# Group-norm statistics of five samples: two small matrix products replaced by a store, a spread load and VectorE sums

## What is computed

```
# per sample; x, ctx: (512, 2048); q = layernorm(x)
t = Wt @ ctx;  p = Wp @ q;  g = Wg @ ctx
# 8 groups of 64 channels
att = sum over the group's channels and columns of p * g     # one number a group
y   = Wz_group @ (att * t_group)
mu, var = mean and variance of y over the group's 64 channels and 2048 columns
x  = x + (y - mu) * rsqrt(var + eps) * gn_w + gn_b + ctx
# feed-forward: layernorm over columns, rows gathered by a permutation,
# 16 heads: gelu(rows @ up[h]) @ down[h], scattered back and added
out = x + ffn(layernorm(x))
```

## Time and profile before

| | us |
|---|---|
| median of three runs | 1517.67 |
| lowest and highest of the three | 1512.51, 1521.18 |
| span of the profiled execution, first to last instruction | 1516.6 |
| PE busy | 1496.1 |
| PEld, DVE, ACT, POOL busy | 1233.7, 1192.4, 1065.8, 962.8 |

### The profile page before, as it was taken

How to read it: one execution, slowest core, us unless ns; L and a number is a source line. 1 busy time by engine, 2 the same in 40 slices (tenths; PEclk the granted TensorE clock), 3 DMA queues, 4 the chain that set the end, 5 groups by cost and what they waited for, 6 DMA issues and landing times.

```text
span 1516.6 us, 19144 instructions
## 1 busy us (share of the span) xinstructions
PE 1496.1 (99%) x6592; PEld 1233.7 (81%) x6592; DVE 1192.4 (79%) x1514; ACT 1065.8 (70%) x1321; POOL 962.8 (63%) x765
## 2 busy tenths in 40 slices
PE   8999999998999999999999999999999999999998
PEld 7878888887888888888888888888888888777886
DVE  4989868875788767887678877888778876889876
ACT  4636757844878568784687847878378773899876
POOL 1673686297862668626784357834579355898887
PEclk9999999999999999999999999999999999999999
DMA  9998788786677936778376784767747776768886
GB/s 327 330 379 332 229 301 298 269 265 204 202 264 266 276 118 221 246 262 278 119 237 248 246 260 133 261 237 250 231 146 275 249 237 204 236 197 257 289 285 221
DMA packets 166865, 374.76 MB, mean 247 GB/s; under 512 B 14960, under 2 KB 80496, under 8 KB 158576
## 3 DMA queue, kind: packets, MB, share of 16 engines
q1 hardware_dynamic: 141424, 281.25, 56.3%
q0 software_dynamic: 25344, 92.29, 17.3%
HBM read 287.45 MB, written 86.03 MB: 246 GB/s over the span
## 4 chain that ended last, share of the span: by engine, by line
PE 80%; DVE 4%; POOL 4%; DMA 4%; ACT 3%; issue 3%; SPq 0%; POOLq 0%; ACTq 0%; DVEq 0%
PE PP L892 13%; PE PP L938 12%; PE PP L953 12%; PE PP L896 6%; PE PP L941 6%; PE PP L957 6%; PE PP L879 6%; PE PP L880 6%; PE PP L874 6%; PE PP L909 4%; PE PP L913 2%; POOL out L1346 1%; POOL FB L1338 1%; POOL FB L1341 1%; ACT Z L1031 1%
## 5 line engine op out<-in xcount | busy, mean ns | idle before, releaser
L938 PE MATMUL PP<-GG,WW 128*128 128x512 f32 x1008 | 270.5, 390 | 4.4 <-issue 4.4
L1046 ACT ACTIVATE PP<-PP 128x1024 f32<-128x1024 f32 x256 | 262.0, 1024 | 0.0
L1249 DVE TENSOR_TENSOR R<-PP,R 128x1024 fp32r<-128x1024 f32 x175 | 213.6, 1220 | 52.5 <-ACT PP L1046 50.6
L892 PE MATMUL PP<-R,WC 128*128 128x512 f32 x1024 | 253.1, 389 | 0.7 <-ACT Z L998 0.7
L1330 POOL TENSOR_TENSOR X<-X,RAW 128x512 f32<-128x512 f32 x112 | 189.2, 1725 | 96.4 <-DVE bn L1069 71.6
L1045 ACT ACTIVATE R<-PP 128x1024 fp32r<-128x1024 f32 x175 | 180.1, 1029 | 87.5 <-PE PP L941 86.5
L938 PEld LDWEIGHTS PP<-GG,WW 128*128 128x128 f32 x1008 | 189.6, 188 | 44.4 <-issue 4.8
L892 PEld LDWEIGHTS PP<-R,WC 128*128 128x128 f32 x1024 | 192.1, 188 | 41.0 <-ACT Z L998 1.1
L1084 DVE TENSOR_TENSOR R<-RAW,R 128x1024 fp32r<-128x1024 f32 x128 | 184.1, 1445 | 49.8 <-ACT R L976 49.8
L1346 POOL DMA_INDIRECT out<-FB,perm_sb x128 | 153.4, 1198 | 82.0 <-DVE FB L1255 64.1
L1323 POOL DMA_INDIRECT FB<-xg_scratch,perm_sb x128 | 127.7, 997 | 115.1 <-DMA xg_scratch<-FB 74.4
(11 more groups left out here) (122 smaller groups left out, 2582.5 us busy)
## 6 DMA issues: line engine op xcount, KB each, us to landing
WW<-w_scratch SPq DMA_DIRECT2D x148, 512.0 KB
X<-in_x SPq DMA_DIRECT2D x32, 1024.0 KB, 6.0
RAW<-in_cx SPq DMA_DIRECT2D x32, 1024.0 KB
RAW<-in_xT SPq DMA_DIRECT2D x63, 512.0 KB
RAW<-in_cT SPq DMA_DIRECT2D x63, 512.0 KB
xg_scratch<-FB SPq DMA_DIRECT2D x104, 256.0 KB
w_scratch<-WW POOLq DMA_DIRECT2D x16, 1024.0 KB, 6.8
HX<-wp_scratch SPq DMA_DIRECT2D x7, 1024.0 KB, 8.2
```

The costliest lines, as they stand in the source:

```text
L892: eng.matmul(PP[2 + ot // 2][:, ot % 2, :], WC[:, l, ct, part(ot)], u[:, ct, :], start=(l == 0 and ct == 0), stop=False)
L938: eng.matmul(pp[:, e, :], wt[:, l, part(2 * p + e)], g[:, 0, :], start=(l == 0), stop=False)
L1046: eng.activation(pp[:], pp[:], ACT.Gelu).then_inc(S["gelu"], 1)
L1249: eng.tensor_tensor(h_tile(f, p, 1), PP[slot["up", f, p]][:], f32(h_tile(f, p, 0)), ALU.subtract).then_inc(S["hlo"], 1)
```

## The change

For samples 2 to 6 (`LOCAL`) the two products with `avg` are gone, and with them `g_mean` and `g_var_a`. In their place:

- att, mean and variance of each channel are written side by side into one tile `st` (all samples, so the copy L1143 falls away for all of them).
- `store_st` (SP, f0 + 0.6) stores `st` to HBM, 12 numbers from each partition.
- `spread_st` (SP, f0 + 4.5) reads them back with two transfers, one a group half: each partition gets the 768 numbers of its own 64 partitions. They go into the `RAW` buffer that held Wg.
- `g_local` (DVE, f0 + 12.3) has eight instructions: it sums the 768 numbers to 12, scales the means, subtracts the mean from 256 numbers, squares them, sums them to 4, and makes var times att squared in three instructions of 4 numbers each.
- `g_root` moves to f0 + 12.4, `g_var_b` and `mean_x1` to f0 + 14.25.

Samples 0, 1 and 7 keep the two products.

```diff
+LOCAL = (2, 3, 4, 5, 6)
...
-        put(f0 + 1.2, g_mean_mm, i)
-        put(f0 + 1.25, g_mean, i)
-        put(f0 + 2.3, g_var_mm, i)
-        put(f0 + 2.35, g_var_a, i)
-        put(f0 + 2.4, g_root, i)
-        put(f0 + (3.9 if first else 5.25), g_var_b, i)
+        if i in LOCAL:
+            put(f0 + 0.6, store_st, i)
+            put(f0 + 4.5, spread_st, i)
+            put(f0 + 12.3, g_local, i)
+            put(f0 + 12.4, g_root, i)
+            put(f0 + 14.25, g_var_b, i)
+        else:
...
+            elif stage == "g_local":
+                i = a[0]
+                gst = S["gst"]
+                all_st = st_tile(i).rearrange("p (k t j) -> p k t j", t=NT, j=3)
+                diff = RAW[slot["wg", i]][:, 2, 0:64 * NT].rearrange("p (k t) -> p k t", t=NT)
+                square = RAW[slot["wg", i]][:, 3, 0:64 * NT].rearrange("p (k t) -> p k t", t=NT)
+                dve.wait_ge(*at["stl", i])
+                eng.tensor_reduce(gm[:], all_st.rearrange("p k t j -> p t j k"), AXIS.X, ALU.add).then_inc(gst, 1)
+                dve.wait_ge(*at["gst", i, "gs"])
+                eng.tensor_scalar(gm[:, :, 1], gm[:, :, 1], 1.0 / 64, None, ALU.mult).then_inc(gst, 1)
+                dve.wait_ge(*at["gst", i, "gm"])
+                eng.tensor_tensor(diff, all_st[:, :, :, 1], gm[:, :, 1].unsqueeze(1).broadcast_to([P, 64, NT]),
+                                  ALU.subtract).then_inc(gst, 1)
+                dve.wait_ge(*at["gst", i, "diff"])
+                eng.tensor_tensor(square, diff, diff, ALU.mult).then_inc(gst, 1)
+                dve.wait_ge(*at["gst", i, "square"])
+                eng.tensor_reduce(gsq[:], square.rearrange("p k t -> p t k"), AXIS.X, ALU.add).then_inc(gst, 1)
...
+            elif stage == "store_st":
+                i = a[0]
+                sp.wait_ge(*at["att", i, NT - 1])
+                sp.wait_ge(*at["mvy", i, NT - 1])
+                eng.dma_start(st_d[i][:, :], st[:].rearrange("p t j -> p (t j)")).then_inc(S["stw"], 16)
+            elif stage == "spread_st":
+                i = a[0]
+                sp.wait_ge(*at["stw", i])
+                for t in free["stl", i]:
+                    sp.wait_ge(*t)
+                for g in range(2):
+                    eng.dma_start(st_tile(i)[64 * g:64 * g + 64, :],
+                                  st_d[i][64 * g:64 * g + 64, :].rearrange("k j -> (k j)").partition_broadcast(64)).then_inc(
+                        S["stl"], 16)
```

More of the change, by code:

```diff
@@ L249, in aggr_y @@
         free["mvy", i] = take(("mvy",))
-        for ot in range(NT + 1):
+        for ot in range(NT):
             n.up("mvy", i, ot)
@@ L293, in g_bank, with store_st, spread_st, g_local @@
         return (3, 1) if i == 0 else (1, 1)
+    def store_st(i):
+        give(n.dma("stw", i), ("att",), ("mvy",))
+        order.append(("store_st", i))
+    def spread_st(i):
+        free["stl", i] = take(("raw", slot["wg", i]))
+        n.dma("stl", i, count=2)
+        order.append(("spread_st", i))
+    def g_local(i):
+        for what in ("gs", "gm", "diff", "square", "squares", "sum", "va"):
+            t = n.up("gst", i, what)
+        give(t, ("raw", slot["wg", i]))
+        n.up("gst", i, "vaa")
+        order.append(("g_local", i))
     def g_mean_mm(i):
@@ L648, in plan @@
         put(v0 + 3.4, aggr_y, i)
-        put(f0 + 1.2, g_mean_mm, i)
-        put(f0 + 1.25, g_mean, i)
-        put(f0 + 2.3, g_var_mm, i)
-        put(f0 + 2.35, g_var_a, i)
-        put(f0 + 2.4, g_root, i)
-        put(f0 + (3.9 if first else 5.25), g_var_b, i)
+        if i in LOCAL:
[5 more added lines that the diff above has]
+        else:
+            put(f0 + 1.2, g_mean_mm, i)
+            put(f0 + 1.25, g_mean, i)
+            put(f0 + 2.3, g_var_mm, i)
+            put(f0 + 2.35, g_var_a, i)
+            put(f0 + 2.4, g_root, i)
+            put(f0 + (3.9 if first else 5.25), g_var_b, i)
         last = i == B - 1
@@ L664, in plan @@
                 put(t + 0.1, load_x, i + 1, ct)
-        put(f0 + (4.1 if first else 5.26), mean_x1, i)
+        put(f0 + (14.26 if i in LOCAL else 4.1 if first else 5.26), mean_x1, i)
         e = f0 + 12 if first else f0 + 22.8 if last else base[i + 1] + 8.6
@@ L800, in build_in @@
     vs_d = nc.dram_tensor("vs_scratch", [B, C], F32, kind="Internal")
+    st_d = [nc.dram_tensor(f"st_scratch{b}", [P, 3 * NT], F32, kind="Internal") for b in range(B)]
     vq_d = nc.dram_tensor("vq_scratch", [B, 4, 2, P], F32, kind="Internal")
@@ L1138, in vector @@
                 for ot in range(NT):
[L1139 to L1143, removed]
+                    eng.bn_aggr(st[:, ot, 1:3], bny[:, ot, :]).then_inc(S["mvy"], 1)
             elif stage == "v_att":
@@ L1152, in vector @@
                                          scalar=0.0, op0=ALU.mult, op1=ALU.add,
-                                         accum_out=am[:, 0, ot:ot + 1]).then_inc(S["att"], 1)
+                                         accum_out=st[:, ot, 0:1]).then_inc(S["att"], 1)
             elif stage == "g_mean":
@@ L1177, in vector @@
                 dve.wait_ge(*at["gpw", i, 1])
-                eng.tensor_tensor(sm[:, 0, :], rs[:, 2, :], sm[:, 3, :], ALU.mult).then_inc(gst, 1)
+                att = gm[:, :, 0] if i in LOCAL else sm[:, 3, :]
+                eng.tensor_tensor(sm[:, 0, :], rs[:, 2, :], att, ALU.mult).then_inc(gst, 1)
                 dve.wait_ge(*at["gst", i, "r"])
```

31 lines of the change are left out of this document (20 added, 11 removed).

## The result

| | before | after |
|---|---|---|
| median of seven runs, us | 1520.27 | 1532.37 |
| lowest and highest, us | 1512.51, 1522.85 | 1527.57, 1538.19 |
| profiled execution, us (its span) | 1517.67 (1516.6) | 1536.16 (1534.3) |

The ratio is 1.0086, with a 95% interval of 1.0065 to 1.0108. So the change costs some 13 us (10 to 16), where I had forecast a gain of 2.6. The time lies outside my range.

The account below looks back on a forecast made before the run. PE was taken to bound the kernel by its large products. Removed 2.6 us (five samples of 0.51) and added 0, so 1517.67 - 2.6 = 1515.1 us, chance 0.50, range 1511 to 1523 us.

Parts of the forecast that it names:

- What bounds the kernel: In samples 2 to 6, PE's 816 large products times their pace make 185.0 of the 185.4 to 185.5 us.
- the first term: On PE, removing the two small products saves 0.51 us a sample, 2.6 us over five samples.
- Transfers at zero: store_st and spread_st on SP cost nothing, with some 14 us of cover before g_local reads the data.
- G = 3.6: Length of g_local on VectorE in us, between an h_lo and add_r; ends 3.1 (never held) and 5.7 (held twice).
- Rival two: g_local's wide steps cost as much again a number, 1.3 us; PE stalls 1.1 us a sample, 1520.6 us; chance 0.20.
- The half microsecond of holding: In g_local, the tensor_scalar is held by POOL's addition L1341 until about 396.9, half a microsecond more.
- The limit of 3.8 us: PE is not held at the L957 behind g_local while g_local takes up to 3.8 us.
- I expect 3.6 + 1.66 = 5.3. No stall, 0.5 us to spare.: g_local plus g_var_b and mean_x1 on VectorE together stay under 5.76 us, so PE does not stall.
- The term for g_var_b and mean_x1: One h_lo behind g_local on VectorE: 1.66 us as at the old place; 0.95 if not held, 2.2 if held.
- from there POOL stands at g_root and holds nobody: After L1341 ends near 396.9, POOL waits at g_root and holds no VectorE instruction; no cost added.
- rival one: POOL isn't early, so its addition holds g_local to 4.8 us; five stalls of 0.3 to 1.0 us, 1516.6 to 1520.1; chance 0.20.
- The limit of 5.76 for both stages: g_local plus g_var_b and mean_x1 may take 5.76 us before PE is held at the L957 at 406.32.

Follow-up runs that it names:

- experiment 3: Kernel before without the two small products in samples 2 to 6 and without any averaging in their place; ratio 0.9997 to the kernel before, samples of 184.96 us.
- experiment 11: Changed kernel with g_local in four pieces from f0 + 8.3, g_root at f0 + 28.9, g_var_b and mean_x1 at f0 + 30.25; ratio 0.9984 to the kernel before.
- experiment 7: Kernel before, products kept, with store_st and spread_st added and their data unread; ratio 0.9990 to the kernel before, samples of 185.46 us.
- experiment 2: Changed kernel with the two sums and the difference of g_local reading neighbouring numbers; ratio 1.0062 to the kernel before, samples of 186.93 us.
- Experiment 4: Kernel before, products kept, with g_root, g_var_b and mean_x1 of samples 2 to 6 at the changed kernel's places; ratio 1.0006 to the kernel before.
- experiment 1: Changed kernel with g_var_b and mean_x1 of samples 2 to 6 at f0 + 20.25 instead of f0 + 14.25; ratio 1.0055 to the kernel before.
- experiment 12: Changed kernel, g_local in one piece, with g_root at f0 + 28.9 and g_var_b and mean_x1 at f0 + 30.25; ratio 1.0014 to the kernel before.
- Experiment 9: Kernel before with 2.8 us of unread POOL work added at f0 + 12.4 of samples 2 to 6; ratio 1.0070 to the kernel before.
- experiment 8: Kernel before, products kept, with the transfers and g_local added, its results unread and POOL not waiting for it; ratio 1.0057 to the kernel before.
- experiment 6: Changed kernel with g_local in three pieces from f0 + 8.3, g_root at f0 + 14.9, g_var_b and mean_x1 at f0 + 20.25; ratio 1.0035 to the kernel before.

## Why the prediction was wrong

- **What bounds the kernel, and the first term: right.** PE's number of products times their pace. The small products are worth 0.49 us a sample (I said 0.51), shown by the traces of experiments 3 and 11. The times alone don't show it.
- **Transfers at zero: right**, by experiment 7. The spread's two transfers were issued from 374.0 on in sample 2 and landed within 5.7 us, some 20 us ahead of their reader.
- **G = 3.6: 3.92.** POOL was early, as I said. The strides cost 0.88 us: 3.1 (my lower end, never held) + 0.88 = 3.98. Rival two had this mechanism, with 1.3 us instead of 0.88. The Trainium skill, page "SBUF — State Buffer", section "Specifications (TRN2)", has a line rule, by which each step to a new line costs. The trace agrees in direction: 0.80 ns more a number at a step of 48 bytes. The half microsecond of holding that I had put in didn't come, since the longer first sum outlasted the addition; where the sum was short, in experiment 2, the tensor_scalar was held. So the two misses offset each other in part. The limit of 3.8 us was right as well: 0.12 over it gave a stall of 0.17.
- **The step that failed: "I expect 3.6 + 1.66 = 5.3. No stall, 0.5 us to spare."** The term for g_var_b and mean_x1, 1.66 us with ends of 0.95 and 2.2, measured 3.73. I took its price from the old place, and looked for POOL's additions only around g_local. Two instructions were held, by two additions one behind the other, and my upper end had one. Experiment 4 has 3.35 to 3.43 us at that place, with the products in and no g_local. With G = 3.92 this alone would be some 1.5 us over the limit, an estimate from these numbers. This is the first and largest part of the loss, 1.81 us a sample, and experiment 1 removes it.
- **A second step, priced at nothing: "from there POOL stands at g_root and holds nobody".** True for as long as it stands. But it stands for 2.6 us, works 1.4 more, and then has its two additions to do. I gave no reason for putting this at nothing. Against experiment 4 it makes g_var_b longer by some 0.4 us. It also makes POOL late, and so does g_local, whose late add_r the scatter waits for. Where no stall at g_var_b gives POOL time to catch up, g_root at this place costs 0.9 us a sample late in the block (1.49 in experiment 1, 0.55 in experiment 12). In the changed kernel PE's own stall at g_var_b hides most of that (across it POOL's lateness falls from 1.7 to 0.9 us in samples 3 and 4), and the 0.65 us of later steps are little more than the 0.55 that g_local brings without it in experiment 12. That PE's stall is what hides it is argued from these numbers, and not shown. I had the row for it in my hand: rival one says that a step takes POOL 5.41 us and PE 5.44, so it catches up by 0.03 us a step. I used it for POOL's place at g_local, and not for what comes behind. Experiment 9 shows that a late POOL alone costs time, and in experiment 11 it isn't late and the loss is gone.
- **The limit of 5.76 for both stages: right.** 7.65 - 5.76 = 1.89, and 1.98 were measured.
- **Rivals.** The time rose, as in rival two, and beyond its 1520.6 us, but mainly through g_var_b, which no case of mine had. Rival two's strides are real and made only a part of it. Rival one's mechanism is real (experiment 8), but its condition, a POOL that isn't early, wasn't met.

What stays open: which late step stalls in which sample. In one kernel samples of the same program differ by up to 2.5 us (experiment 6: 185.00 and 187.43), and no run here says why one sample stalls and the next doesn't. The table is a correlation over fourteen kernels, and only experiment 9 sets the lateness by itself. No run has g_var_b at its new place behind g_local with a POOL that isn't held up at all, so the shares of the 1.81 us are not shown one by one.

## What to carry over

An engine that is idle for 40% of the time may have no reserve in the stage that counts. By the windows of the kernel before, POOL is busy for 72.5 of the 87.1 us of the sixteen steps (sample 4), and for 39.0 of the 98.4 us of the rest. So compare its step with the bound engine's step, here 5.41 against 5.44 us, and count work or a wait that is put on it there as lost until something gives it back. Place a small step on such an engine where its result is next needed and its input long done, not right behind the producer. A price that was read at the old place holds for the old place: where work is moved, look for what runs beside each item that moves with it, at its new place and after the shift that the move itself makes.

## What the runs showed of the hardware

- A VectorE sum of 768 float32 numbers takes 942 ns when they are neighbours, and 1559 ns at a step of 12 numbers; of 256 numbers 420 ns, and 609 at a step of 4. A two-operand instruction of 256 numbers takes 426 ns contiguous and 498 with one operand at a step of 3.
- A VectorE instruction that reads two tensors from SBUF and a POOL addition hold each other. Four numbers took 1.97 us and 512 numbers up to 2.40 us instead of 0.15 and 0.68. A tensor_scalar of four numbers, which reads one tensor, was held too: 0.32 us in experiment 8 and 0.61 in experiment 2, instead of 0.17. A POOL addition of 1.30 us took 1.63 or 1.64 when g_lo stood beside it, and 2.16 in experiment 9 beside an L1092 (819.10). The long sum wasn't held: it took 1.56 us beside an addition, and the addition beside it 1.30.
- An instruction that has begun is held as well. In all these traces a g_lo that began during the gather took 0.63 to 0.71 us when the next addition began more than 0.7 us later, and 1.9 to 2.5 us when it began within 0.66 us. L1227 of four numbers was held by an addition whose record starts 0.65 us after its own, and no run says why so short an instruction was not done by then.
- Both meeting in successive steps can go on: POOL's step was then 5.49 us against 5.44 in experiment 1, so that POOL didn't get away from g_lo.
